# A state-space layer on one core: step size as four more columns of the gate's projection, multiplied into the rows of x by ScalarE; segment sums in two banks; calls in a new order

## The reference, cut to what matters

```
zxbcdt = einsum('bld,ed->ble', u, W_in)        # 256 z, 512 xBC, 4 dt
z   = zxbcdt[..., :256];  xBC = zxbcdt[..., 256:768]
dt  = softplus(zxbcdt[..., 768:] + dt_bias)    # step size, one for each of 4 heads
xBC = silu(conv_b + causal convolution of xBC over 4 tokens)
x, B, C = xBC[..., :256] (4 heads x 64), xBC[..., 256:384], xBC[..., 384:]
dA  = exp(dt * -exp(A_log))
h_t = h_{t-1} * dA_t + (dt_t * x_t) outer B_t  # for each head
y_t = h_t C_t + x_t * D
g   = y * silu(z);  g = g * rsqrt(mean(g * g) + eps) * norm_w
out = einsum('ble,de->bld', g, W_out)
```

## Time and profile before

| what | value |
| --- | --- |
| median of 3 runs | 790.94 us (790.15 to 792.07) |
| the profiled execution | 789.89 us |
| its span | 788.2 us |
| mean granted TensorE clock | 0.975 of full speed |
| PE, PEld, DVE, ACT, POOL busy | 94%, 76%, 83%, 69%, 34% |

### The profile page before, as it was taken

The page is one execution under the profiler, slowest core; times in us unless marked ns, Lnnn a source line. Parts: engine busy times, 40 slices in busy tenths (PEclk is TensorE's granted clock), DMA queues, the critical chain, the costliest instruction groups (busy, mean ns, idle before and its releaser), DMA issues.

```text
span 788.2 us, 15048 instructions
## 1 busy us (share of the span) xinstructions
PE 740.8 (94%) x3896; PEld 600.2 (76%) x3896; DVE 654.1 (83%) x1612; ACT 544.5 (69%) x934; POOL 270.9 (34%) x417
## 2 busy tenths in 40 slices
PE   4899998889999999989999999899978899999997
PEld 3588786668788888768888888788766688888885
DVE  2578887979998999758789998899859799999996
ACT  2676766777888888665566576466548787888885
POOL 2345553701111012024747657556644011111010
PEclk9999999989999999999999999999969899999999
DMA  8000001535555555100000000000035456656651
GB/s 256 1 1 3 5 2 45 217 134 186 193 179 196 185 184 180 56 1 1 1 2 2 3 3 2 3 2 0 3 109 173 140 188 203 192 193 207 204 191 60
DMA packets 29218, 76.95 MB, mean 98 GB/s; under 512 B 4883, under 2 KB 9454, under 8 KB 29166
## 3 DMA queue, kind: packets, MB, share of 16 engines
q1 hardware_dynamic: 29012, 76.36, 29.3%
q10 hardware_dynamic: 154, 0.00, 0.0%
HBM read 73.73 MB, written 2.62 MB: 97 GB/s over the span
## 4 chain that ended last, share of the span: by engine, by line
PE 74%; DVE 9%; issue 8%; POOL 4%; DMA 2%; ACT 1%; SPq 1%; POOLq 0%; DVEq 0%; ACTq 0%
PE ps L1577 7%; PE ps L1578 7%; PE ps L1579 7%; PE ps L1558 7%; PE ps L1559 7%; PE ps L1560 7%; PE ps L1417 3%; PE ps L1384 3%; PE ps L1607 2%; PE ps L1609 2%; PE ps L1608 2%; PE ps L1409 2%; PE ps L1717 2%; PE ps L1694 2%; DVE s_lo L1116 1%
## 5 line engine op out<-in xcount | busy, mean ns | idle before, releaser
L744 ACT ACTIVATE s_ring<-ps,b1T 128x512 f32<-128x512 f32 x256 | 172.7, 689 | 73.3 <-PE ps L1579 72.2
L1150 DVE SCALAR_TENSOR_TENSOR s_ring<-s_ring,top_col,r_all 128x1024 f32<-128x1024 f32 x128 | 174.2, 1361 | 38.6 <-ACT s_ring L744 35.1
L1116 DVE TENSOR_TENSOR s_lo<-s_ring,s_hi 128x1024 fp32r<-128x1024 f32 x128 | 165.1, 1290 | 0.0
L732 ACT ACTIVATE s_hi<-s_ring 128x1024 fp32r<-128x1024 f32 x128 | 134.4, 1050 | 1.8 <-DVE s_ring L1150 1.8
L1577 PE MATMUL ps<-ffn_hi,w_hi 128*128 (+1 forms) x256 | 105.5, 412 | 1.0 <-issue 1.0
L454 POOL CAST rows_r<-rows_f 80x512 fp32r<-80x512 f32 x16 | 15.7, 979 | 262.3 <-DMA rows_f<-route_dram 262.3
L1558 PE MATMUL ps<-s_hi,w_hi 128*128 128x512 f32 x256 | 102.5, 401 | 1.4 <-DVE s_lo L1116 1.4
L1579 PE MATMUL ps<-ffn_hi,w_lo 128*128 (+1 forms) x256 | 102.9, 402 | 0.0
L1578 PE MATMUL ps<-ffn_lo,w_hi 128*128 (+1 forms) x256 | 102.8, 402 | 0.0
L1559 PE MATMUL ps<-s_lo,w_hi 128*128 128x512 f32 x256 | 102.3, 399 | 0.0
L1560 PE MATMUL ps<-s_hi,w_lo 128*128 128x512 f32 x256 | 102.0, 398 | 0.0
(11 more groups left out here) (235 smaller groups left out, 1611.9 us busy)
## 6 DMA issues: line engine op xcount, KB each, us to landing
r_all<-route_dram SPq DMA_DIRECT2D x128, 512.0 KB, 4.3
out_dram<-X SPq DMA_DIRECT2D x8, 256.0 KB, 4.8
X<-in_L_attn_a_x_dram SPq DMA_DIRECT2D x1, 1536.0 KB, 10.4
rows_f<-route_dram SPq DMA_DIRECT2D x48, 32.0 KB, 2.7
w_rows<-in_L_ffn_mlp_w_dram SPq DMA_DIRECT2D x1, 1024.0 KB, 6.8
route_dram<-route_cols SPq DMA_DIRECT2D x64, 8.0 KB, 1.5
X<-in_L_attn_a_x_dram SPq DMA_DIRECT2D x2, 256.0 KB, 3.2
in_rows<-in_L_attn_b_W_in_dram SPq DMA_DIRECT2D x1, 384.0 KB
```

The costliest lines, as they stand in the source:

```text
L732: eng.activation(s_hi[:, q % NR, :, :], s_ring[:, q % NR, :, :], ACT.Copy).then_inc(F["hi"], 1)
L744: eng.activation(s_ring[:, q % NR, e % 2, :], bank(e % 4), ACT.Silu, bias=b1T[:, e:e + 1], scale=ALPHA).then_inc(F["act"], 1)
L1116: eng.tensor_tensor(s_lo[:, q % NR, :, :], s_ring[:, q % NR, :, :], s_hi[:, q % NR, :, :].bitcast(F32), ALU.subtract).then_inc(F["lo"], 1)
L1150: eng.scalar_tensor_tensor(out=s_ring[:, q % NR, :, :], in0=s_ring[:, q % NR, :, :], scalar=top_col[:, 0:1], in1=r_all[:, q % NR, :, :], o ...
```

## The change

Four things change, all in the SSM.

1. The four columns of dt are put behind the 256 of z: zT has 260 columns, `dt_proj` and its bank are gone, and `z_proj` is one product of 260 columns for each chunk, alternately in banks 6 and 7. `z_out` is one copy of 260 columns for each chunk in place of one of 512 for two. `dt_arg` reads dt from zs. So the gate's projection now comes ahead of `project_in`, straight behind `u_low`.
2. `xb_out` copies B by one instruction and then the rows of x by four, one for each head, with dt as the scale. xb_tok now holds dt * x. `grams` loses to_end and is one instruction of 512 columns, segs * cb. `weigh` reads its factor from the last column of segs.
3. `cb_of` writes to the last quarter of bank 0, whose first three quarters `xb_turn` fills; bank 1 becomes free and the segment sums alternate between banks 1 and 2. Both `cb_of` and `xb_turn` now wait until `cb_out` and `xb_out` of the chunk before are done, and `xb_out` waits for `cb_out`.
4. The calls in `step` stand in a new order on all four engines.

```diff
-                eng.activation(xb_tok[:, c % 2, :, :], bank(1)[:, 0:3 * P]..., ACT.Copy).then_inc(M["xb"], 1)
+                wait(eng, M["cb"], n + 1)
+                wait(eng, M["dt"], b + 1)
+                eng.activation(xb_tok[:, c % 2, 2, :], bank(0)[:, 2 * P:3 * P], ACT.Copy)
+                for h in range(NH):
+                    x_rows = eng.activation(xb_tok[:, c % 2, h // 2, (h % 2) * HD:(h % 2 + 1) * HD],
+                                            bank(0)[:, h * HD:(h + 1) * HD], ACT.Copy, scale=dt_a[:, par, 0, c, h:h + 1])
+                x_rows.then_inc(M["xb"], 1)
...
             def grams(b, par, c):
                 wait(eng, M["segs"], n + 1)
-                wait(eng, M["xw"], (NT - 1) * b + max(c - 1, 0))
-                eng.tensor_tensor(to_end[:, c % 2, :], segs[:, c % 2, :, P - 1], dt_a[:, par, 0, c, :],
-                                  ALU.mult).then_inc(M["end"], 1)
                 wait(eng, M["cb"], n + 1)
                 wait(eng, M["y_ps"], n - 1)
-                for h in range(NH):
-                    eng.scalar_tensor_tensor(out=gram[:, c % 2, h, :], in0=segs[:, c % 2, h, :],
-                                             scalar=dt_a[:, par, 0, c, h:h + 1], in1=cb[:, c % 2, :], ...)
+                eng.tensor_tensor(gram[:, c % 2, :, :], segs[:, c % 2, :, :],
+                                  cb[:, c % 2, :].unsqueeze(1).to_broadcast([P, NH, P]), ALU.mult).then_inc(M["gram"], 1)
...
             def project_in(b, k):
                 wait(eng, M["u_lo"], b + 1)
-                if k == 1:
-                    wait(eng, F1["acc_sb"], NB)
-                    wait(eng, M["xs"], 3 * b)
+                wait(eng, M["z_raw"], NT * b + NT - k)
...
             def z_proj(b, c):
                 wait(eng, M["u_lo"], b + 1)
+                if c == 0:
+                    ...
+                    wait(eng, M["xs"], 3 * b)
+                elif c > 1:
+                    wait(eng, M["z_raw"], NT * b + c - 1)
                 at = PAD + c * P
-                mm = product(bank(6 + k)[:, c % 2 * DI:(c % 2 + 1) * DI], ...)
+                product(bank(6 + c % 2)[:, 0:DI + NH], parts_of(uT, slice(at, at + P)), parts_of(zT, slice(None))).then_inc(M["z_ps"], 1)
-            def dt_proj(b):
-                wait(eng, M["u_lo"], b + 1)
-                wait(eng, M["state"], (NT - 1) * (b - 1) + 1)
-                for c in range(NT):
-                    mm = product(bank(4)[:, c * NH:(c + 1) * NH], ..., parts_of(dtT, slice(None)))
-                mm.then_inc(M["dt_ps"], 1)
...
             def cb_of(b, par, c):
                 if c == 0:
-                    wait(eng, M["xs"], 3 * b + 3)
+                    wait(eng, M["xs"], 3 * b + 2)
                 wait(eng, M["cb"], n)
-                eng.matmul(bank(0)[:, 0:P], xs[:, par, 2, at], xs[:, par, 3, at], ...).then_inc(M["cb_ps"], 1)
+                wait(eng, M["xb"], n)
+                eng.matmul(bank(0)[:, 3 * P:], xs[:, par, 2, at], xs[:, par, 3, at], start=True, stop=True)
...
             def seg_sum(b, c):
-                wait(eng, M["segs"], n)
+                wait(eng, M["segs"], n - 1)
                 wait(eng, M["ramp"], n + 1)
-                eng.matmul(bank(2), after[:, :], ramp...)
+                eng.matmul(bank(1 + c % 2), after[:, :], ramp...)
```

More of the change, by code:

```diff
@@ L540, in step @@
                 if second:
-                    fade(i, odd, 2)
-                    weigh(i, odd, 2)
+                    gate(i, odd, 0)
+                    fade(i, odd, 1)
                 if fourth:
@@ L1302, in step @@
                 if second:
-                    grams(i, odd, 1)
-                    ys(i, odd, 0)
+                    grams(i, odd, 0)
                 if third:
                     x3_out(i - 1, 4)
+                if second:
+                    cb_out(i, 1)
                 if first:
@@ L1311, in step @@
                 if second:
-                    states(i, 0)
+                    grams(i, odd, 1)
+                    ys(i, odd, 0)
+                if fourth:
+                    router_lg(R2, i - 2, bank(5)[:, 0:NT * NE])
+                if second:
+                    states(i, 0)
+                    cb_out(i, 2)
+                if fourth:
+                    router_top(R2, i - 2)
+                if first:
+                    dt_arg(i + 1, 1 - odd)
+                if second:
+                    grams(i, odd, 2)
                 if first:
@@ L1770, in step @@
                 if second:
-                    cb_of(i, odd, 1)
-                    seg_sum(i, 1)
+                    xb_turn(i, odd, 0)
+                    y_skip(i, odd, 0)
+                if fourth:
+                    router_turn(R2, i - 2, 5, lambda: wait(eng, M["gT"], least(NT * i, NT * NB)))
                 if third:
                     out_proj(i - 1, 4)
+                if first:
+                    u_turn(i + 1)
                 if second:
+                    cb_of(i, odd, 1)
                     xb_turn(i, odd, 1)
                     y_gram(i, 0)
+                if first:
+                    z_proj(i + 1, 0)
+                    z_proj(i + 1, 1)
+                if second:
+                    next_state(i, 0)
+                if fourth:
+                    router_logits(R2, i - 2, bank(5), lambda: None)
+                if second:
                     cb_of(i, odd, 2)
+                    xb_turn(i, odd, 2)
                 if first:
-                    u_turn(i + 1)
-                if fourth:
-                    router_turn(R2, i - 2, 5, lambda: wait(eng, M["gT"], least(NT * i, NT * NB)))
+                    z_proj(i + 1, 2)
+                    z_proj(i + 1, 3)
                 if second:
                     seg_sum(i, 2)
-                    y_skip(i, odd, 1)
                 if first:
@@ L1788, in step @@
                 if second:
-                    next_state(i, 0)
-                    xb_turn(i, odd, 2)
+                    y_skip(i, odd, 1)
+                    y_state(i, odd, 1)
+                    y_gram(i, 1)
+                    next_state(i, 1)
+                    cb_of(i, odd, 3)
+                    xb_turn(i, odd, 3)
                 if first:
                     project_in(i + 1, 1)
-                    dt_proj(i + 1)
                 if second:
-                    y_state(i, odd, 1)
-                    cb_of(i, odd, 3)
-                    xb_turn(i, odd, 3)
-                    y_gram(i, 1)
-                    next_state(i, 1)
-                if fourth:
-                    router_logits(R2, i - 2, bank(5), lambda: None)
-                if second:
-                    seg_sum(i, 3)
                     y_skip(i, odd, 2)
@@ L1806, in step @@
                     y_gram(i, 2)
+                    seg_sum(i, 3)
+                    next_state(i, 2)
+                    g_turn(i, 0)
                 if first:
@@ L1809, in step @@
                 if second:
-                    next_state(i, 2)
+                    y_skip(i, odd, 3)
+                    y_state(i, odd, 3)
                 if first:
```

202 lines of the change are left out of this document (79 added, 123 removed).

## The result

The changed kernel takes 779.84 us (median of 4 runs, 777.32 to 780.08) beside 791.31 us for the kernel before (4 runs, 790.15 to 792.07). The ratio is 0.9854, with a 95% interval from 0.9833 to 0.9875: 1.5% faster. The forecast of 781.0 us was 1.2 us too high. The profiled execution took 779.74 us, with a span of 778.0 us.

A forecast was written before the change was run, and what follows sets the result against it. TensorE was taken as the bound, with VectorE just in time. Steps 0 to 4 and 6 (-7.2), 5 (-1.2), -1 (+0.7) and 7 (-1.3) gave 9.0 us less than 789.89, so 781, range 777 to 787.

The forecast's parts named there:

- no change: Rival for the SSM loop: VectorE and GpSimd hold the step, so the 1.2 us become a wait; 790 us, chance 0.05.
- dt's projection: TensorE in the SSM: dt's twelve matmuls go, 1.23 us less of its stream a step, all on the path.
- grams: VectorE: one 512-column instruction at 0.68 us, 0.53 less a call, 2.1 a step; by itself hidden behind TensorE.
- xb_out: ScalarE: five instructions take 1.1 us (bounds 0.8 and 1.3), 2.4 more a step, hidden as load.
- the slower rival: Shared bank in the SSM: TensorE stands at cb_of in each chunk, 0.4 us a chunk; about 794 us, chance 0.07.
- The step: One step of the SSM loop: 28.0 to 28.5 us, taken as 1.2 us less.
- the segment sums: TensorE in the SSM: two banks take away a wait of some 0.1 to 0.3 us a step, within 0.28 idle.
- The places in the step: Tightest places in an SSM step: TensorE waits 0 to 0.3 us at u_turn and at the gate's products.
- Step 5: Second iteration of the hardware loop: 1.2 us less (0.3 to 2.3), with VectorE's standstill of about 3.2 us staying.
- Step -1: SSM step without chunks to hide anything: 0.7 us lost (bounds -0.8 and +2), convolution 2.4 later.
- Step 7: Tail of the SSM with nothing to fill: 1.3 us less, bounds +0.5 and -3.
- The table load: ScalarE ahead of z_silu: 1.28 us without drain; a drain of about 1.38 could cost about 1 us in all.

The follow-up runs named there:

- dt_back: Changed kernel with twelve products of 4 columns a step put back behind the gate's, their result unread: 790.46 us, ratio 0.9988 to the kernel before.
- gram4: Changed kernel with gram in four instructions of 128 columns again: 784.07 us, ratio 0.9915 to the kernel before.
- before_dt3: Kernel before, with dt from three matmuls of 16 columns in place of twelve of 4: 790.11 us, ratio 1.0009.
- before_both: Kernel before, with dt times x by ScalarE, one gram instruction and dt from three matmuls, in the old order: 790.74 us, ratio 1.0004.
- before_rows: Kernel before, with only dt times x by ScalarE, one gram instruction and no to_end: 791.02 us, ratio 1.0005.
- seg_one: Changed kernel with the segment sums in one bank, the second sum behind y_skip and the first seg_exp moved: 785.26 us, ratio 0.9941 to the kernel before.
- xb_one: Changed kernel with x and B copied in one instruction again, leaving dt out of x: 777.49 us, ratio 0.9854 to the kernel before.
- both_banks: Same edits to the kernel before as before_both, plus B.C, x and B of a chunk sharing a bank, alternately 0 and 1: 794.73 us, ratio 1.0053.
- tail: Changed kernel with GpSimd's router_chain of the last SSM step moved behind rms(2): 777.08 us, ratio 0.9839 to the kernel before.

## Why the prediction was right

**The bound.** That TensorE is the bound was right for the changed kernel: dt_back costs 1.27 to 1.34 a step for 1.25 priced. It is not the only one: VectorE's four instructions put back cost 0.7 to 0.85 (gram4). For the kernel before it was half the truth. There TensorE was full, and the other engines' path was as long: before_dt3 took 0.94 us a step of matmuls away and nothing came of it. The rival "no change" (a ring of the other engines holds the step) would have been right for the first edit alone.

**dt's projection.** 1.23 a step priced. In the table it is 1.25 gone, and the gate's projection has not grown but shrunk by 0.22. "All of it lies on the path" holds with the new order and banks, and not without them (before_dt3, before_both).

**grams.** 0.68 taken, 0.69 measured. "By itself it is hidden behind TensorE": true by itself (before_rows), but gram4 shows 0.7 to 0.85 a step for it in the changed kernel. The gains are not a sum; each of dt_back, gram4 and seg_one gives back 0.65 to 1.34 a step, out of the same 1.5 to 1.9.

**xb_out.** 1.1 taken, 1.09 measured; that the shared bank is hidden in the loop was right (xb_one), and no wait for cb or xb_tok shows there. That rules out the slower rival here; both_banks shows its mechanism, a shared bank with calls in an order that doesn't suit it.

**The step.** Here the size was off. 1.2 less was taken, for 28.0 to 28.5 a step; steps 0 to 4 and 6 give 9.8 in all and not 7.2, so 1.64 in the mean, and steps 3, 4 and 6 take 27.4 to 27.8. The term that was too small is that of the segment sums: I looked for a gain only in TensorE's idle time (0.28) and put 0.1 to 0.3 on it, within that. The wait of 0.26 for segs is gone (it stands in the row of B.C, 0.32 less), and the sums took 0.34 less of the stream besides. Going back to one bank with the pair split costs 0.65 to 0.8 a step (seg_one). In the other rows of step 4 gains and losses nearly cancel (gate and skip 0.52 less, gram by x and next state 0.55 more). Busy time hid it: the profile counts part of what a stream loses between two groups as busy.

**The places in the step.** u_low was to be done 7.2 to 7.7 us into the step: it ends at 465.08, 7.25 after cb_of, and TensorE waited 0.24 there (0 to 0.3 said).

**Step 5.** -1.2 taken, -1.04 measured. The standstill stays, 3.02 us (about 3.2 said).

**Step -1.** +0.7 taken, +0.95 measured, with the convolution 2.8 later (2.4 said). The low clock came too, for 3.4 us.

**Step 7.** -1.3 taken, -0.77 measured. fade(1) stands behind router_chain on GpSimd, from which a wait of 1.89 us for the state came. The order around router_chain was named and its price was not worked out. But tail took that wait away and the step did not get shorter, so the wait is not shown to be the 0.5 us that are missing. The clock was also low for less time, 10.2 us in place of 13.7.

**The table load.** The Trainium skill (ScalarE: Activation LUTs, What ACT_TABLE_LOAD costs) has a drain beside the load. As in the kernel before, the trace has none: 1.28 us, and the next instruction 0.01 behind it. Going by the row was right.

Sum of the SSM: -10.7 where -9.0 was said; +0.4 in the rest, so 10.2 less of span. The forecast lies 1.2 us above the median because of the steps of the loop (2.6 too little), against which step 5, step -1 and step 7 stand (0.9 too much), and so does the 0.5 outside the SSM. That it came so close is in part luck: these errors go against each other.

## What to carry to other kernels

Where two engines are both full, take work from both and then ask again what is queued behind what. Here each of the two parts alone gave nothing, both together in the old order gave nothing, and with the new order and the second bank for the segment sums they gave 11 us. Twelve small products put back took 9.4 us in the steps 0 to 6, while the rest of the program moved by some us with the clock. So set the steps that you edited beside each other, and not only the totals. To price an edit on the bound engine, add up start-to-start distances by group; busy and idle time don't show what is lost between groups. When a PSUM bank is shared to free another, look for the instruction that now waits for the later of the two writers, and move that writer forward.

## What the hardware showed that was not expected

- Twelve matmuls with 4 columns, spread between the gate's products, took 1.01 us, and the gate's products with them 0.17 more: 0.10 each, as in the earlier trace rows. Three with 16 columns took 0.25.
- At the second iteration of the hardware loop VectorE stood still for 3.02 us in the changed kernel and for 3.23 in the kernel before. Written out, the same step has no such gap, and takes 4.2 us less.
- The clock in the 20 us of step -1 differs from trace to trace: 0.92 and 0.91 in the two stretches before, 1.00 and 0.87 after, 0.71 and 0.64 with twelve small products more, 1.00 and 1.00 with project_in first. It is 1.00 in gram4 too, where step -1 has the same work in the same order as after. With one trace of each, it is not shown how much of this the edits brought about.
- Where router_norm's first instruction on VectorE started while GpSimd's ramps ran, it lasted until 0.08 us after the end of ramps, in 25 of 25 cases: 0.41 to 0.86 us in place of 0.34. So the first half of router_norm took 1.56 us in place of 1.11. The next three ran beside GpSimd's ln_rs without such an effect, and cb_out ran beside ramps in its usual 0.29.
